# Tokenizer of a vision tower: phase products on GpSimd, 11 of 16 tokens summed on TensorE, zero streams among the products

## The reference, cut to what matters

```python
dt = jnp.exp(log_dt)
dtA = A * dt[:, None]
Ct = B[None] * C / (1.0 - dtA / 2) * dt[:, None]
dA = (1.0 + dtA / 2) / (1.0 - dtA / 2)
dA_log = jnp.log(dA)
l = jnp.arange(L, dtype=jnp.float32)
V = jnp.exp(dA_log[:, :, None] * l)
K = 2.0 * jnp.einsum('chn,hnl->chl', Ct, V).real
```

## Time and profile before

| | |
|---|---|
| median of 3 runs | 1677.65 us (1675.43, 1677.65, 1681.29) |
| span of the profiled execution, first to last instruction | 1675.7 us |
| the profiled execution's own time | not listed apart from its span |
| tokenizer, first instruction to last product | 0 to 221 us |
| its loop over chunks | 71 to 221 us |
| busy share of the span: PE, PEld, DVE, ACT, POOL | 88%, 59%, 76%, 60%, 35% |
| granted TensorE clock, mean of the span | 0.907 of 2.4 GHz |

### The profile page before, as it was taken

The page is one execution under the profiler, slowest core; times in us unless marked ns, Lnnn a source line. Parts: engine busy times, 40 slices in busy tenths (PEclk is TensorE's granted clock), DMA queues, the critical chain, the costliest instruction groups (busy, mean ns, idle before and its releaser), DMA issues. The chain is left out here.

```text
span 1675.7 us, 30721 instructions
## 1 busy us (share of the span) xinstructions
PE 1477.0 (88%) x11240; PEld 988.9 (59%) x11326; DVE 1271.8 (76%) x2388; ACT 1003.2 (60%) x2539; POOL 580.4 (35%) x600
## 2 busy tenths in 40 slices
PE   2099967999999999999978877779999599999997
PEld 2099945677666677666656666566765244444443
DVE  8999936777777777777753346359999599999996
ACT  7799817887787887788862224178886223333331
POOL 0000004445445554445440000017777433333332
PEclk9555568999999999999998799989999799999998
DMA  2022242322333332333345026177885244444443
GB/s 82 1 51 63 64 146 84 106 93 94 106 119 102 93 94 93 106 112 100 99 145 190 1 90 235 47 223 208 209 219 141 59 105 99 102 102 103 101 101 82
DMA packets 233095, 183.01 MB, mean 109 GB/s; under 512 B 163568, under 2 KB 165104, under 8 KB 232944
## 3 DMA queue, kind: packets, MB, share of 16 engines
q1 hardware_dynamic: 232944, 181.03, 37.7%
HBM read 93.95 MB, written 59.77 MB: 92 GB/s over the span
## 5 line engine op out<-in xcount | busy, mean ns | idle before, releaser
L1059 PE MATMUL al_ps<-w,al_xT 128*128 128x512 f32 (+2 forms) x1024 | 351.6, 497 | 0.0
L1059 PEld LDWEIGHTS al_ps<-w,al_xT 128*128 128x128 f32 x1024 | 192.3, 193 | 127.2 <-issue 107.3
L2213 POOL TENSOR_TENSOR ff_zq<-ff_z,ff_back 128x1024 bf16<-128x1024 fp8e4 x64 | 122.6, 1915 | 223.3 <-DVE ff_z L2237 223.3
L450 PE MATMUL tk_ps<-tk_w,tk_l 128*128 128x64 f32 x512 | 119.6, 422 | 57.8 <-DVE tk_w L419 51.0
L2179 ACT ACTIVATE ff_sg<-af_ps 128x1024 f32<-128x1024 f32 x64 | 65.5, 1024 | 150.7 <-PE af_ps L2262 150.7
L450 PEld LDWEIGHTS tk_ps<-tk_w,tk_l 128*128 128x128 f32 x512 | 114.2, 332 | 60.4 <-issue 60.4
L754 POOL TENSOR_TENSOR al_qv<-al_qv,al_qe 128x512 f32<-128x512 f32 x48 | 63.1, 1315 | 234.7 <-PE al_ps L1118 234.7
L2262 PE MATMUL af_ps<-wgT,xqT 128*128 128x512 bf16 x500 | 122.1, 384 | 14.4 <-ACT ff_sg L2179 13.6
L2283 PE MATMUL af_ps<-wdT,ff_zT 128*128 128x512 bf16 x504 | 123.6, 387 | 5.8 <-DMA ff_zT<-ff_zq 5.3
L2262 PE MATMUL af_ps<-wuT,xqT 128*128 128x512 bf16 x502 | 121.4, 382 | 6.5 <-DVE ff_z L2229 3.9
L2034 PE MATMUL af_ps<-ag_w,ag_aT 128*128 128x512 f32 x256 | 112.6, 593 | 1.7 <-ACT af_ps L1870 1.7
(11 more groups left out here) (298 smaller groups left out, 3388.0 us busy)
## 6 DMA issues: line engine op xcount, KB each, us to landing
al_hx<-h_s SPq DMA_DIRECT2D x36, 256.0 KB, 2.8
o_s<-al_o SPq DMA_DIRECT2D x32, 272.0 KB, 2.2
h_s<-tk_w SPq DMA_DIRECT2D x16, 512.0 KB, 3.8
v_s<-al_v SPq DMA_DIRECT2D x32, 256.0 KB, 2.2
k_s<-al_kT SPq DMA_DIRECT2D x32, 256.0 KB, 2.4
q_s<-al_qT SPq DMA_DIRECT2D x32, 256.0 KB, 2.6
lt_k<-k_s SPq DMA_DIRECT2D x16, 512.0 KB, 5.1
lt_v<-v_s SPq DMA_DIRECT2D x16, 512.0 KB, 3.6
```

The lines of the kernel that those rows point to most:

```text
L450: ins = pe.matmul(o, L[:, u, 0, t], R[:, u, t], start=True, stop=t < CS)
L1059: ins = pe.matmul(out, xT[:, T, k], w[:, k, cols], start=False, stop=True, skip_group_check=True)
L2213: pool.tensor_tensor(zq[:, u].rearrange("p (k s) -> p k s", s=QB), z8[:, u].rearrange("p (k s) -> p k s", s=QB), back[:, u, :, None].to_br ...
```

## The change

- `CS` goes from 13 to 5: VectorE's addition covers 5 tokens (128 by 640) and not 13 (128 by 1664), and TensorE makes two products for 11 tokens and not for 3.
- The products frequency times a move from ScalarE to GpSimd: one instruction for a whole chunk, with both inputs broadcast (`raw_ready`). ScalarE adds the offset with one instruction for the chunk, in place. GpSimd's instruction for chunk ch waits for `nf_ready` of chunk ch - 2, whose buffer it writes.
- A tile of zeros (`still`) is laid over the coefficients `bri`, once these have been read; VectorE clears it in the first stage.
- TensorE streams these zeros, 128 by 512 in bf16, through the identity into the unused bank `ps[4]`: 24 times ahead of the first chunk (after `s_pb`), and behind every second token of each chunk.

```diff
-    CS = 13
+    CS = 5
+        still = bri[:].rearrange("p a n r -> p (a n r)").bitcast(BF16)
             def phases(ch):
-                if ch >= 2:
-                    act.wait_ge(nf_ready, ch - 1)
-                for t in range(CH):
-                    ins = act.activation(ph[:, ch % 2, t], c("iota_a"), ACT.Identity,
-                                         scale=par[:, 1, ch * CH + t:ch * CH + t + 1], bias=c("off_r"))
-                ins.then_inc(ph_ready, 1)
+                act.wait_ge(raw_ready, ch + 1)
+                act.activation(ph[:, ch % 2], ph[:, ch % 2], ACT.Identity, bias=c("off_r")).then_inc(ph_ready, 1)
...
-            act.wait_ge(s_par, 2)
+        @block.gpsimd
+        def _(pool):
+            pool.wait_ge(s_ld, 80)
+            pool.wait_ge(s_xd, 4)
+            pool.wait_ge(s_par, 2)
+            for ch in range(NCH):
+                if ch >= 2:
+                    pool.wait_ge(nf_ready, ch - 1)
+                t0 = ch * CH
+                pool.tensor_tensor(ph[:, ch % 2], par[:, 1, t0:t0 + CH, None].to_broadcast([P, CH, 64]),
+                                   c("iota_a")[:, None, :].to_broadcast([P, CH, 64]), ALU.mult).then_inc(raw_ready, 1)
...
-            st.mark(dve.tensor_copy(K.identb[:], c("ident")))
+            dve.memset(still, 0.0).then_inc(s_still, 1)
+            dve.tensor_copy(K.identb[:], c("ident")).then_inc(s_idb, 1)
...
+            def stream():
+                pe.matmul(ps[4][:], K.identb[:], still, start=True, stop=True)
+            pe.wait_ge(s_still, 1)
+            pe.wait_ge(s_idb, 1)
+            pe.wait_ge(s_pb, 1)
+            for _ in range(24):
+                stream()
             for ch in range(NCH):
...
                     if t >= CS:
                         ins = pe.matmul(o, L[:, u, 1, t], R[:, u, t], start=False, stop=True)
+                    if t % 2 == 0:
+                        stream()
```

More of the change, by code:

```diff
@@ L178, in tokenizer @@
         s_pb = sem("tk_pbd")
+        s_still, s_idb = sem("tk_stilld"), sem("tk_idb")
+        raw_ready = sem("tk_raw_ready")
         ph_ready = sem("tk_ph_ready")
```

## The result

The changed kernel takes **1767.78 us** (median of 4 runs, 1762.77 to 1770.89), against 1677.22 us for the kernel before in runs beside it (4 runs, 1675.43 to 1681.29). The ratio is 1.053, with a 95% interval of 1.0506 to 1.0555: some 90 us slower, where 23 us had been forecast. The sign was right, and so were GpSimd's hold on VectorE and the fall of the clock; that the clock would come back was wrong. The size was that of the third rival, whose case reached up to 1770.

A forecast was written before the change was run, and what follows sets the result against it. Tokenizer loop bound equally by VectorE's work (8.63 us a chunk) and ScalarE's chain (8.83). With the clock up +6, three low-clock chunks +17: +23 on 1675.7, plus 1.95, gives 1701 us; range 1654 to 1728.

The forecast's parts named there:

- The sign: Whole kernel: slower than before, by 23 us or 1.4%; chance of slower 0.70.
- GpSimd's hold on VectorE: Tokenizer loop: each GpSimd chunk product makes VectorE wait 1.68 us, so a chunk takes 9.24 us.
- the fall of the clock: Tokenizer loop: TensorE's pause of 1.64 us a chunk sometimes drops its clock to 1.2 GHz, 5.76 us more per chunk.
- that the clock would come back: Tokenizer loop: streams among the products raise the clock again after some time, so three low chunks, +17 us.
- the third rival: Tokenizer loop: clock falls early and stays down, seven to fifteen low chunks, +46 to +92, 1724 to 1770 us; chance 0.20.

The follow-up runs named there:

- One kernel: The changed kernel with CS = 0, all sixteen tokens summed on TensorE: eight of ten executions 1672.48 to 1681.94 us, two 1793.66 and 1796.76.

## What to carry to other kernels

Work moved to GpSimd is not off the path if VectorE runs two-input SBUF instructions beside it: price it on VectorE in full, and compare with VectorE doing it itself (here 1.71 against 1.22 us). Where a gain hangs on TensorE's clock, make TensorE the engine without pauses first, and count its chunk at both levels; a loop that has a state in which it feeds itself is to be priced all or nothing, with a chance for each, not by a number of bad turns in the middle, unless a row of that loop shows the way back. And before streams are added to hold the clock, look for a row in which that very mixture raised it: streams that don't are paid at the low clock's price.

## What the hardware showed that was not expected

- GpSimd's waiting instruction gets in between two VectorE instructions that follow each other without a wait: 3.88 us for 1.91 of work, and the second of the two VectorE instructions grew by 1.70.
- A small VectorE instruction pays as much as a large one: 0.29 became 1.99 us for 256 elements a row, its operands from one tile.
- At 1.2 GHz, streams of 512 columns behind every second token left the clock low for 211 us of a full TensorE, and behind every token the clock rose in 4 us.
- One kernel had two times, around 1678 and 1795 us. In the one trace there is, of a long execution, the clock fell 1.6 us behind a pause of 1.56 us at the loop's start and stayed down.
